# One kernel of convolutions, masked operations and filters: the next layer's code is read inside the running operation

## The chip, the cores and the metric

The kernel runs on one core of a Trainium2 chip. The core has TensorE (PE, matrix products, with its weight loads as PEld), VectorE (DVE), ScalarE (ACT), GpSimd (POOL) and SyncE (SP), each with its own stream of instructions; they meet at semaphores. The metric is the device time of one execution in microseconds (us), the median over runs.

## The reference

The input `x` has four images of 32 channels and 28 x 28 points in float32. Four stages follow one another, each a residual over a norm:

```python
x = x + conv_block(ln_channels(x))          # 1x1 and 3x3 convolutions, two L1-distance convolutions
t = to_tokens(x)                            # (4, 784, 32)
t = t + scan(ln_tokens(t))                  # 33 layers, see below
x = from_tokens(t)
x = x + quantised_convs(ln_channels(x))
t = to_tokens(x); t = t + spectral_filters(ln_tokens(t))
```

The change lies in the scan. Each of its 33 layers does this:

```python
op = argmax(h[0, 0, :19])                    # one token decides for all
y  = softmax(q @ k.T * scale) @ v @ wo[op]   # q, k, v = h @ wq[op], ...
h  = where(attn_mask[layer, op], y, h)
z  = relu(h @ w1[op] + b1[op]) @ w2[op] + b2[op]
h  = where(ffn_mask[layer, op], z, h)
```

The masks are mostly false, so that a layer may do nothing, an attention, an FFN, or both.

## The kernel before, in words

**Layout.** The four images lie side by side on the 128 partitions (32 channels each), the 784 points in the free dimension, mostly handled as two halves of 392. A product in float32 is two passes of PE, so the profile counts two per matmul. PSUM has eight banks.

**The scan as a program of jumps.** DVE keeps a table of which layers are active for which op. Once the first token of H is known, it works out the next active layer and its code (bit 0 attention, bit 1 FFN, above them the layer and the op) and writes it into KINT, one integer in SBUF: `decide` (L885 to L898, the last instruction a cast into KINT), which raises the semaphore `decided`. Before that it has made ready what can follow, in `past` and `look_ahead` (from L717 and L708). Every engine reads KINT into a register with a TENSOR_LOAD and jumps. `active_steps` builds the body of a layer, `step`, three times on each engine: for the first layer, the second, and in a loop for all further ones. With these inputs two layers are active: the first does an FFN only, so that PE, ACT and DVE jump over the attention's code, the second an attention and an FFN. Then the code is zero, and all jump to the exit.

**Around it on PE.** The LayerNorm ahead (`norm(1, ...)`) centres X1 by products with CEN, sums squares by products with VSEL, and spreads the reciprocal deviations RSC by eight products with CON and SPR; DVE multiplies them into H (L653). PE then waits for H, reads the code (L1249) and jumps. `keep_warm(n)` is n products of constants into an unused bank, which nobody reads; `bridge` is one product with a single column that carries a wait.

**The FFN.** A one-column product for the deciding token; eight hidden units HIDT (two halves by four images, numbers 0 to 7), each one product with W1R into a bank, evicted with bias and relu by ACT (0, 2, 3, 4, 6; L561) or DVE (1, 5, 7; L995); between units 3 and 4 the token's own row, from which DVE decides the next layer; then two groups of four output products with W2S (L1408 to L1410), which ACT evicts to the halves of H (L565). PE then adds two products CEN by X1 into banks 4 and 5, the first part of the third LayerNorm, should this layer be the last. SyncE waits for `decided`, and fetches the weights of the next operation: W4R (attention), W1R and W2S (FFN).

**The attention's end.** Scores, exponentials (ACT, PT), and products with the values VT run in fourteen steps. The sum of the exponentials (the denominator) comes from products with ones: DVE adds the first of a chunk in ACC (L965), PE sums the others and then ACC into bank 7. DVE takes the reciprocal (L981), PE multiplies the values' sum NUM by W4R, DVE scales the result into H (L984), and decides again.

Every engine has its order written out by hand; what runs when follows from these orders and the semaphores.

## Time and profile before

| | |
|---|---|
| median of 3 runs | 344.49 us (344.34 to 348.11) |
| profiled execution | 343.95 us, its span 342.2 us |
| PE busy | 322.1 us (94%), in 5173 passes |
| DVE, ACT busy | 249.4 us (73%), 188.6 us (55%) |
| granted clock of PE | nine tenths or more in all 40 slices |

Times in the trace count from the span's start. The span holds what the engines do; the rest of the execution lies around it. The scan starts at about 140 us and the third LayerNorm ends at about 232 us. A matmul's end is modelled, so PE counts as busy while passes are in flight.

### The profile page before, as it was taken

What the parts mean: (1) busy time and instruction counts of PE and PEld (TensorE: products, weight loads), DVE (VectorE), ACT (ScalarE), POOL (GpSimd) and SP (SyncE); (2) the same over time, 40 slices, a digit from 0 to 9 for tenths busy, and PEclk for the clock granted to TensorE, in tenths of its full rate; (3) what the DMA queues carried; (4) which work ended last, traced back from release to release, by engine and by line L of the source; (5) the groups of instructions that cost most, each with busy time, mean ns of one, the idle gap of its engine ahead of it and who ended that gap; (6) DMA issues with size and microseconds to landing.
All of it is one profiled execution on the core that took longest, in us unless ns stands there. A gap on an engine that the chain in (4) does not pass through costs nothing.

```text
span 342.2 us, 11955 instructions
## 1 busy us (share of the span) xinstructions
PE 322.1 (94%) x5173; PEld 202.4 (59%) x5173; DVE 249.4 (73%) x510; ACT 188.6 (55%) x214; POOL 21.5 (6%) x48
## 2 busy tenths in 40 slices
PE   8899799999999999958999999989899999999995
PEld 7436437763333333434465334446589999999984
DVE  2797999999999999544694877647657675564444
ACT  3871898887889894324584867641333323223221
POOL 4573000000000000300000000000000000000000
PEclk9999999999999999999999999999999999999999
DMA  5701820000000003700000000000023000000001
GB/s 181 234 17 20 310 99 2 2 1 2 2 2 2 2 2 111 268 14 19 3 0 2 3 1 2 2 5 1 2 61 87 7 4 4 4 5 4 6 4 50
DMA packets 12243, 13.20 MB, mean 39 GB/s; under 512 B 6026, under 2 KB 10908, under 8 KB 12184
## 3 DMA queue, kind: packets, MB, share of 16 engines
q1 hardware_dynamic: 11208, 9.17, 9.0%
q0 software_dynamic: 832, 3.00, 2.6%
q8 instruction: 43, 0.70, 0.9%
q10 hardware_dynamic: 144, 0.20, 0.2%
q14 instruction: 16, 0.13, 0.1%
HBM read 10.73 MB, written 0.40 MB: 33 GB/s over the span
## 4 chain that ended last, share of the span: by engine, by line
PE 54%; DVE 31%; SPq 7%; issue 4%; ACT 2%; DVEq 1%; DMA 1%; ACTq 0%
PE PS L1088 54%; DVE pool_ L877 18%; SPq L274 3%; DVE pool_ L965 1%; DVE TMP L841 1%; DVE TMP L973 1%; SPq L268 1%; DMA WA2R<-in_wa2r 1%; SPq L277 1%; SPq L279 1%; DVE RSC L648 1%; DVE pool_ L874 1%; SPq L281 1%; DVE MSC L790 1%; ACT pool_ L544 0%
## 5 line engine op out<-in xcount | busy, mean ns | idle before, releaser
L1088 PE MATMUL PS<-pool_,CON 128*32 128x392 f32 (+2 forms) x1320 | 111.4, 493 | 0.6 <-ACT pool_ L544 0.2
L1088 PEld LDWEIGHTS PS<-pool_,CON 128*32 128x32 f32 (+1 forms) x1320 | 49.0, 110 | 60.8 <-issue 43.7
L495 ACT ACTIVATE pool_<-TMP,WA 128x3136 f32<-128x3136 f32 x26 | 75.3, 2924 | 11.0 <-PE PS L1088 10.8
L877 DVE TENSOR_SCALAR pool_<-TMP,WA 128x3136 f32<-128x3136 f32 x44 | 79.4, 1845 | 0.1
L594 ACT ACTIVATE pool_<-PS 128x272 f32<-128x272 f32 x64 | 25.4, 398 | 56.7 <-PE PS L1088 56.6
L1061 DVE TENSOR_TENSOR pool_<-PS,pool_ 128x128 f32<-128x128 f32 x64 | 18.6, 290 | 35.4 <-PE PS L1088 32.7
L1088 PE MATMUL PS<-HE,WS 128*32 128x136 f32 (+1 forms) x768 | 36.7, 317 | 0.2 <-ACT WS L586 0.2
L1088 PE MATMUL PS<-pool_,WS 128*32 128x136 f32 (+1 forms) x768 | 36.7, 316 | 0.0
L1088 PEld LDWEIGHTS PS<-pool_,WS 128*32 128x32 f32 x768 | 28.7, 109 | 3.0
L1088 PEld LDWEIGHTS PS<-HE,WS 128*32 128x32 f32 x768 | 28.3, 110 | 3.6 <-issue 0.6
L1088 PE MATMUL PS<-pool_,TMP 128*32 128x128 f32 x512 | 29.0, 272 | 0.0
L1088 PE MATMUL PS<-CON 128*128 128x196 f32 (+1 forms) x112 | 21.7, 332 | 4.3 <-issue 3.8
L544 ACT ACTIVATE pool_<-PS 112x896 f32<-112x896 f32 (+1 forms) x28 | 21.5, 820 | 6.1 <-PE PS L1088 6.1
L1088 PEld LDWEIGHTS PS<-CON 128*128 128x128 f32 x112 | 18.1, 190 | 10.8 <-issue 8.4
L965 DVE TENSOR_TENSOR pool_<-pool_ 112x1792 f32<-112x1792 f32 (+1 forms) x9 | 16.3, 1810 | 5.1 <-ACT pool_ L544 5.0
L1088 PEld LDWEIGHTS PS<-pool_,TMP 128*32 128x32 f32 x512 | 18.9, 109 | 0.0
L1062 DVE TENSOR_TENSOR pool_<-PS,pool_ 128x136 f32<-128x136 f32 x64 | 18.5, 288 | 0.0
L1064 DVE TENSOR_TENSOR pool_<-PS,pool_ 128x128 f32<-128x128 f32 x64 | 17.9, 280 | 0.0
L1088 PE MATMUL PS<-QZ,Y 32*112 32x448 f32 (+1 forms) x112 | 15.2, 532 | 0.7 <-ACT pool_ L544 0.7
L944 DVE CUSTOM_DVE_ANT_0 pool_<-PS,pool_ 112x392 f32<-112x392 f32 x28 | 13.8, 561 | 2.3 <-ACT pool_ L525 2.3
L1088 PE MATMUL PS<-pool_,ASEG 128*32 128x49 f32 (+2 forms) x512 | 14.6, 247 | 0.2 <-DVE pool_ L1064 0.2
L1088 PE MATMUL PS<-Y,QZ 32*112 32x392 f32 x56 | 14.0, 529 | 0.0
(261 smaller groups left out, 372.3 us busy)
## 6 DMA issues: line engine op xcount, KB each, us to landing
pool_<-in_pho SPq DMA_DIRECT2D x1, 3144.0 KB, 10.7
HE<-in_phe SPq DMA_DIRECT2D x1, 3136.0 KB, 12.5
QZ<-CW SPq DMA_DIRECT2D x12, 98.0 KB, 2.4
CW<-in_cw POOLq DMA_DIRECT2D x2, 576.0 KB, 4.8
CON<-in_con POOLq DMA_DIRECT2D x1, 732.5 KB, 5.4
out_y<-Y SPq DMA_DIRECT2D x1, 392.0 KB, 2.4
CQ<-in_ws SPq DMA_DIRECT2D x16, 9.0 KB
MPP<-in_mpp POOLq DMA_DIRECT2D x1, 256.0 KB, 2.9
```

Of the source, the lines that this page charges most:

```text
L268: sp.dma_start(PAR[q, 0:PC["cb"]], rows_).then_inc(s["par_in"], 16)
L274: sp.dma_start(WS2N[32 * b + 8 * g:32 * b + 8 * g + 8, :, :], bass.AP(ws2.tensor, (32 * g + 8 * b) * 9 * P + C * b, [[9 * P, 8], [P, 9], [ ...
L495: a.activation(unit, window(n // CQ), ACT.Abs, bias=WA2[:, n:n + 1], scale=-1.0).then_inc(s["act_unit"], 1)
L544: a.activation(PT[0:QT, st % PR, 2 * pair:2 * pair + 2, 0:QC[ch]], PS[0:QT, 2 * ((u + 2) % 3):2 * ((u + 2) % 3) + 2, 0:QC[ch]], ACT.Exp, s ...
L594: a.activation(spans(UEV[:, u % 8, :], 2 * P), spans(PS[:, 2 * (u % 3), :], QE), ACT.Copy).then_inc(s["uev_act"], 1)
L877: v.tensor_scalar(unit, window(n // CQ), WA2[:, n:n + 1], None, ALU.max).then_inc(s["dve_unit"], 1)
L944: v.tensor_tensor_reduce(RISE[0:QT, j % 2, b, :], PS[0:QT, b, 0:HT], RISE[0:QT, j % 2, b, :], 1.0, -3.4e38, ALU.add, ALU.max, TOPS[0:QT, j ...
L965: v.tensor_tensor(ACC[0:QT, :, 0:w], PT[0:QT, (st - 1) % PR, :, 0:w] if i == 1 else ACC[0:QT, :, 0:w], PT[0:QT, st % PR, :, 0:w], ALU.add) ...
L1061: v.tensor_tensor(y[:, P:2 * P], low[:, 0:P], y[:, 0:P], ALU.add).then_inc(s["uev_sum"], 1)
L1062: v.tensor_tensor(y[:, 2 * P:NPH], low[:, 0:QE], y[:, 2 * P:NPH], ALU.add).then_inc(s["uev_sum"], 1)
L1064: v.tensor_tensor(y[:, P:2 * P], low[:, QE:QE + P], y[:, P:2 * P], ALU.add).then_inc(s["uev_dve"], 1)
L1088: return t.matmul(out_, lhsT, rhs, start=start, stop=stop, skip_group_check=True)
```

## The change

- **PE and ACT read the next code inside the FFN.** `next_code` stands between the two halves of the output and loads into a second register, `coming`; at the operation's end a register move takes it over. A layer without an FFN reads at its end, under a new condition. DVE and SyncE still read at the end of their step.
- **The first code** is read inside the LayerNorm: on PE after the variance's products, on DVE while it waits for the spreading products. PE's wait for H moves behind the jump, the wait for the evicted H of a layer before the next operation's first product, and for the last layer before the exit's first product.
- **The centring products of X1** move from behind the FFN to between its two output groups; each waits until the hidden unit in its bank is evicted.
- **ACT evicts six units** (0, 1, 2, 3, 4, 6), DVE two (5, 7), and DVE decides before them. The token's row stands after unit 1.
- **The attention's last products:** the sum over ACC comes before the last step's exponentials, which now finish the denominator; the two bridging products at the end become one of 32 columns; the token's row stands before the second output product.
- **Warming:** 3 products instead of 8 before the projections, 1 instead of 2 at the attention's end, and the 8 of the loop's layers go; two of the places use bank 7.
- **FFN code aligned:** the instructions after the first attention's code, where PE's jump over it lands, begin at a multiple of 256 instructions.

PE, the code read ahead of the first operation, before:

```order
L1088 MATMUL PS<-RSC,CON 128x98
L1088 MATMUL PS<-RSC,SPR 128x98
L1249 TENSOR_LOAD KINT [waits decided,ln_out]
L1250 REGISTER_ALU
L109 COMPARE_AND_BRANCH
L82 REGISTER_ALU
L82 COMPARE_AND_BRANCH
```

and now:

```order
L1099 MATMUL PS<-TMP,VSEL 32x98 x3
L1265 TENSOR_LOAD KINT [waits decided]
L1266 REGISTER_ALU
L1099 MATMUL PS<-X,CEN 128x392
L1099 MATMUL PS<-RSC,CON 128x98 [waits ln_rs]
L1099 MATMUL PS<-RSC,SPR 128x98
```

The read stands between the variance's products (TMP by VSEL) and the second centring product; only the branches are left behind the spreading products.

PE, the end of the first FFN, from the first output group on, before:

```order
L1088 MATMUL PS<-pool_,W2S 32x392 x3
L1406 REGISTER_ALU
L1407 REGISTER_ALU [waits hid_act]
L1088 MATMUL PS<-pool_,W2S 32x392 [waits hid_dve]
L1088 MATMUL PS<-pool_,W2S 32x392 x3
L1411 ISA
L1386 UNCONDITIONAL_BRANCH
L1412 ISA
L1088 MATMUL PS<-X,CEN 128x392 x2
L1418 ISA
L1419 REGISTER_ALU [waits ffn_h]
L1421 TENSOR_LOAD KINT [waits decided]
```

and now (the lines of the file have moved; CEN by X are the centring products):

```order
L1099 MATMUL PS<-pool_,W2S 32x392 [waits hid_act]
L1099 MATMUL PS<-pool_,W2S 32x392 x3
L1442 REGISTER_ALU
L1099 MATMUL PS<-X,CEN 128x392 [waits hid_act]
L1099 MATMUL PS<-X,CEN 128x392 [waits hid_dve]
L1273 ISA
L1275 TENSOR_LOAD KINT [waits decided]
L1447 REGISTER_ALU
L1449 REGISTER_ALU [waits hid_act]
L1099 MATMUL PS<-pool_,W2S 32x392 [waits hid_dve]
L1099 MATMUL PS<-pool_,W2S 32x392 x3
L1453 ISA
```

The centring products and the read stand between the two output groups; the wait for ffn_h is gone from here.

PE, the end of the attention, from the last step's sums on (pool_ by CON sums exponentials, pool_ by VT weighs the values, TMP by W4R is the output), before:

```order
L1088 MATMUL PS<-pool_,CON 32x336 [waits exp_done]
L1088 MATMUL PS<-pool_,CON 32x336 x3
L1361 REGISTER_ALU
L1088 MATMUL PS<-pool_,CON 32x336 [waits acc_done]
L1088 MATMUL PS<-pool_,CON 32x336 x3
L1088 MATMUL PS<-pool_,VT 32x336 x4
L1088 MATMUL PS<-CON 128x1 [waits att_scaled]
L1088 MATMUL PS<-TMP,W4R 32x448 x4
L1088 MATMUL PS<-CON 128x1 [waits num_out]
L1088 MATMUL PS<-TMP,W4R 32x336 x4
L1088 MATMUL PS<-W4R,TMP 1x32
```

and now:

```order
L1099 MATMUL PS<-pool_,CON 32x336 x3
L1099 MATMUL PS<-pool_,VT 32x336 x4
L1398 REGISTER_ALU
L1099 MATMUL PS<-pool_,CON 32x336 [waits acc_done]
L1099 MATMUL PS<-pool_,CON 32x336 x3
L1099 MATMUL PS<-pool_,CON 32x336 [waits exp_done]
L1099 MATMUL PS<-pool_,CON 32x336 x3
L1099 MATMUL PS<-pool_,VT 32x336 [waits att_scaled]
L1099 MATMUL PS<-pool_,VT 32x336 x3
L1099 MATMUL PS<-TMP,W4R 32x448 x4
L1099 MATMUL PS<-CON 32x1 [waits num_out]
L1099 MATMUL PS<-W4R,TMP 1x32
```

The sum over ACC (waits acc_done) stands first, the output's first group comes without a bridging product, the token's row (W4R by TMP) before the second group.

The core of the diff:

```diff
-WARM = dict(inputs=6, means=4, squares=2, deviations=3, scaled=4, sums=2, copies=9, evictions=3, shifts=1, relus=3, further=8, rises=2, weights=4, projections=8)
+WARM = dict(inputs=6, means=4, squares=2, deviations=3, scaled=4, sums=1, copies=9, evictions=3, shifts=1, relus=3, further=8, rises=2, weights=4, projections=3)
...
+            def next_code(more):
+
+                a.wait_ge(s["decided"], a.snap(ops, min_val=0, max_val=2 * NB) + more)
+                a.sem_inc(s["read_on"], 1)
+                a.load(coming, KINT[0:1, 0:1], bass_reorder=False)
...
-                    for u in (0, 2, 3, 4, 6):
+                    for u in (0, 1, 2, 3, 4, 6):
...
                     for h in range(2):
+                        if h:
+                            next_code(2)
                         a.wait_ge(s["ffn_out"], k * 2 + (h + 1))
                         a.activation(half(H, h), bank(2 + h), ACT.Identity, bias=B2C[:, :]).then_inc(s["ffn_h"], 1)
                     a.reg_add(nf, nf, 1); a.reg_add(ops, ops, 1)
-                a.wait_ge(s["decided"], a.snap(ops, min_val=1, max_val=2 * NB) + 1)
-                a.sem_inc(s["read_on"], 1)
-                a.load(code, KINT[0:1, 0:1], bass_reorder=False)
-                a.reg_mov(code, a.snap(code) & (OPW - 1))
+                with a.If((c & 2) < 1):
+                    next_code(1)
+                a.reg_mov(code, a.snap(coming) & (OPW - 1))
...
+            norm(1, X1, lambda h: half(H, h), after=first_code)
...
+                    decide(v.snap(ops, min_val=0, max_val=2 * NB) + 2, 7)
+                    for u in (5, 7):
                         v.wait_ge(s["ffn_h1"], k * 8 + (u + 1))
                         v.tensor_scalar(HIDT[:, u, :], bank(u % 7), B1S, 0.0, ALU.add, ALU.max).then_inc(s["hid_dve"], 1)
-                        if u == 1:
-                            decide(v.snap(ops, min_val=0, max_val=2 * NB) + 2, 7)
                     v.reg_add(nf, nf, 1); v.reg_add(ops, ops, 1)
...
+            norm(1, X1, "x1_ready", between=first_code)
...
-                with (t.If((c & 1) > 0) if built else far_unless(t, c & 1, ffn_mark)):
+                with (t.If((c & 1) > 0) if built else far_unless(t, c & 1, ffn_mark, align=True)):
                     k = t.snap(na, min_val=0, max_val=NB)
                     t.wait_ge(s["zeroed"], 4)
-                    keep_warm(WARM["projections"])
+                    keep_warm(WARM["projections"], b=7)
                     t.wait_ge(s["att_w"], k * 16 + 16)
+                    t.wait_ge(s["ffn_h"], t.snap(nf, min_val=0, max_val=NB) * 2 + 1)
+                    if not built:
+                        t.wait_ge(s["ln_out"], 4)
...
-                        if i > ADDS[ch]:
+                        if i > ADDS[ch] and not (ch == 1 and i == NQ - 1):
                             sums(PT[:, st % PR, :, :], i == ADDS[ch] + 1, False)
+                        last_ch = ch == 1
                         if i == NQ - 1:
-                            t.wait_ge(s["acc_done"], k * ADDED[2] + ADDED[ch + 1])
-                            sums(ACC, False, True).then_inc(s["den_done"], 1)
+                            if last_ch:
+                                sums(PT[:, st % PR, :, :], False, True).then_inc(s["den_done"], 1)
+                                t.wait_ge(s["att_scaled"], k + 1)
+                            else:
+                                t.wait_ge(s["acc_done"], k * ADDED[2] + ADDED[ch + 1])
+                                sums(ACC, False, True).then_inc(s["den_done"], 1)
                         for b in range(NIMG):
                             last = mm(bank(6, QC[ch], slice(32 * b, 32 * b + 32)), VT[0:QT, b, C * i:C * i + C],
                                       PT[0:QT, st % PR, b, 0:QC[ch]], i == 0, i == NQ - 1)
                         last.then_inc(s["pv_done"], 1)
+                        if st == 2 * NQ - 2:
+                            t.wait_ge(s["acc_done"], k * ADDED[2] + ADDED[2])
+                            sums(ACC, False, False)
...
-                    t.wait_ge(s["att_scaled"], k + 1)
                     for ch in range(2):
                         if ch:
                             t.wait_ge(s["num_out"], k * 2 + 2)
-                        bridge()
+                            mm(PS[0:C, 3, 0:1], CON[:, 0:C], CON[:, 0:1])
+                            token(NUM[0:C, 0:1], W4R[0:C, 3, :], 6)
                         for b in range(NIMG):
                             q = slice(32 * b, 32 * b + 32)
                             last = mm(bank(ch, QC[ch], q), W4R[q, 3, :], NUM[q, Q0[ch]:Q0[ch] + QC[ch]])
                         last.then_inc(s["att_wo"], 1)
-                    token(NUM[0:C, 0:1], W4R[0:C, 3, :], 6)
                     keep_warm(WARM["sums"])
...
+                        if u == 1:
                             t.wait_ge(s["ffn_wb"], k * 16 + 16)
                             t.wait_ge(s["tok_hid"], k + 1)
...
-                        t.wait_ge(s["hid_act"], k * 5 + 2 * h + 3)
-                        t.wait_ge(s["hid_dve"], k * 3 + 2 * h + 1)
+                        if h:
+                            t.wait_ge(s["hid_act"], k * 6 + 5)
+                            mm(bank(4), CEN[:, :], half(X1, 0), True, False)
+                            t.wait_ge(s["hid_dve"], k * 2 + 1)
+                            mm(bank(5), CEN[:, :], half(X1, 1), True, False)
+                            next_code(2)
+                        t.wait_ge(s["hid_act"], k * 6 + 2 * h + 4)
+                        if h:
+                            t.wait_ge(s["hid_dve"], k * 2 + 2)
                         for b in range(NIMG):
                             last = mm(PS[32 * b:32 * b + 32, 2 + h, 0:HT], W2S[:, 0:C], HIDT[:, 4 * h + b, :])
                         last.then_inc(s["ffn_out"], 1)
                     t.reg_add(nf, nf, 1); t.reg_add(ops, ops, 1)
-                f, o = t.snap(nf, min_val=0, max_val=NB), t.snap(ops, min_val=1, max_val=2 * NB)
-                built.append(o)
-                if len(built) == 3:
-                    keep_warm(WARM["further"])
-                for h in range(2):
-                    mm(bank(4 + h), CEN[:, :], half(X1, h), True, False)
-                t.wait_ge(s["ffn_h"], f * 2 + 1)
-                t.wait_ge(s["decided"], o + 1)
-                t.sem_inc(s["read_on"], 1)
-                t.load(code, KINT[0:1, 0:1], bass_reorder=False)
-                t.reg_mov(code, t.snap(code) & (OPW - 1))
+                with t.If((c & 2) < 1):
+                    for h in range(2):
+                        mm(bank(4 + h), CEN[:, :], half(X1, h), True, False)
+                    next_code(1)
+                built.append(c)
+                t.reg_mov(code, t.snap(coming) & (OPW - 1))
 
             active_steps(t, code, step, exit_marks, align=True)
 
+            t.wait_ge(s["ffn_h"], t.snap(nf, min_val=0, max_val=NB) * 2 + 1)
             for h in range(2):
                 mm(bank(4 + h), CEN[:, :], half(H, h), False, True).then_inc(s["sx_cent"], 1)
             t.wait_ge(s["sx_sq"], 2)
```

## Rows read from the trace of the kernel before

**Rows 1.** The page's chain of waits, whole span, shares by engine.
```profile
PE 54%; DVE 31%; SPq 7%; issue 4%; ACT 2%; DVEq 1%; DMA 1%; ACTq 0%
```
**Rows 2.** Windows: length, busy of PE, PEld, DVE, ACT, POOL, granted clock, DMA.
```profile
147.00:162.40 15.40, 10.59 (x68) 6.54 (x69) 6.77 (x19) 5.27 (x9) 0.00 (x0) 1.00 0.06 13
```
**Rows 3.** Timeline, first operation: start, us, engine, line, operation, [idle before <-releaser].
```profile
144.40 0.46 PE L1088 MATMUL PS<-RSC,CON 128*128 128x98 f32 x2 [0.44 <-DVE RSC L648]
...
146.47 0.56 DVE L653 TENSOR_TENSOR H<-TMP,PS 128x392 f32<-128x392 f32 x1 [0.33 <-PE PS L1088]
148.18 0.14 DVE L717 TENSOR_SCALAR PINT<-KINT 1x1 int32<-1x1 int32 x1 [1.15 <-issue]
...
149.48 1.56 PE L1088 MATMUL PS<-CON 128*128 128x196 f32 x8 [3.05 <-issue]
...
150.97 0.81 PE L1088 MATMUL PS<-H,W1R 32*128 32x1 f32 x3
...
151.76 0.15 DVE L992 COPY B2C<-W1R 128x1 f32<-128x1 f32 x1 [1.17 <-issue]
152.58 0.94 PE L1088 MATMUL PS<-H,W1R 32*128 32x392 f32 x7 [0.79 <-issue]
...
154.08 0.15 DVE L890 TENSOR_REDUCE KMAX<-PS 1x1 f32<-1x19 f32 x1
...
154.84 0.14 DVE L896 CAST KINT<-KMAX 1x1 int32<-1x1 f32 x1
...
156.37 0.87 PE L1088 MATMUL PS<-pool_,W2S 128*32 128x392 f32 x8 [0.73 <-DVE pool_ L995]
...
156.63 0.69 SPq L311 DMA_DIRECT2D W4R<-in_aw  x1
...
159.46 3.01 PE L1088 MATMUL PS<-CON 128*128 128x196 f32 x18 [0.71 <-issue]
...
162.40 2.84 PE L1088 MATMUL PS<-H,W4R 32*32 32x392 f32 x32
```
**Rows 4.** Tile KINT, code reads: engine, operation, ns min/median/max, first and last start.
```profile
L1421 PEldq TENSOR_LOAD <-KINT x2: 312/312/313, 158.2 to 224.6; - x2
...
L1249 PEldq TENSOR_LOAD <-KINT x1: 487/487/487, 147.1 to 147.1; - x1
```
**Rows 5.** DMA queues from 149 to 153 us: kind, packets, MB, share of 16 engines.
```profile
q8 instruction: 1, 0.02, 2.1%
```
**Rows 6.** DMA issues of the whole span: queue, count, KB each, median us to landing.
```profile
QZ<-CW SPq DMA_DIRECT2D x12, 98.0 KB, 2.4
...
W2S<-in_fwb SPq DMA_DIRECT2D x2, 16.5 KB, 2.2
```
**Rows 7.** Timeline, the attention's last products, PE and DVE.
```profile
213.51 1.34 PE L1088 MATMUL PS<-pool_,CON 112*32 112x336 f32 x16 [0.18 <-ACT pool_ L544]
...
215.34 0.38 PE L1088 MATMUL PS<-CON 128*128 128x1 f32 x2
...
217.69 0.51 DVE L984 TENSOR_TENSOR H<-TMP,PS 128x336 f32<-128x336 f32 x1 [0.51 <-PE PS L1088]
```
**Rows 8.** Timeline, the second FFN and the exit, PE and ACT.
```profile
218.77 1.14 PE L1088 MATMUL PS<-H,W1R 32*128 32x1 f32 x10 [0.26 <-issue]
...
219.95 2.50 ACT L561 ACTIVATE pool_<-PS,W2S 128x392 f32<-128x392 f32 x5 [0.51 <-PE PS L1088]
...
219.99 0.21 PE L1088 MATMUL PS<-CON,W1R 32*1 32x32 f32 x2
...
223.62 1.58 PE L1088 MATMUL PS<-X,CEN 128*128 128x392 f32 x4
223.76 0.59 ACT L565 ACTIVATE H<-PS,B2C 128x392 f32<-128x392 f32 x1 [0.62 <-PE PS L1088]
224.93 1.28 ACT L574 ACT_TABLE_LOAD   x1 [0.58 <-issue]
...
226.67 0.50 ACT L407 ACTIVATE TMP<-PS 128x392 f32<-128x392 f32 x1 [0.24 <-PE PS L1088]
```

More of the change, by code:

```diff
@@ L906, in _, with first_code @@
             decide(1, 6)
-            norm(1, X1, lambda h: half(H, h))
+            code = v.alloc_register("v_code"); na = v.alloc_register("v_na"); nf = v.alloc_register("v_nf")
+            def first_code():
+                v.wait_ge(s["decided"], 1)
+                v.load(code, KINT[0:1, 0:1], bass_reorder=False)
+                v.reg_mov(code, v.snap(code) & (OPW - 1))
+            norm(1, X1, lambda h: half(H, h), after=first_code)
             def residual():
                 v.tensor_tensor(X[:, :], X1[:, :], H[:, :], ALU.add).then_inc(s["x2_ready"], 1)
-            code = v.alloc_register("v_code"); na = v.alloc_register("v_na"); nf = v.alloc_register("v_nf")
-            v.wait_ge(s["decided"], 1)
-            v.load(code, KINT[0:1, 0:1], bass_reorder=False)
-            v.reg_mov(code, v.snap(code) & (OPW - 1))
             ops = v.alloc_register("v_ops")
@@ L1113, in spread, with norm @@
                 return last
-            def norm(k, src, ready=None, summed=None):
+            def norm(k, src, ready=None, summed=None, between=None):
                 if k == 1:
@@ L1142, in norm @@
                 last.then_inc(s["ln_var"], 1)
+                if between:
+                    between()
                 rest(k)
@@ L1244, in _, with first_code, next_code @@
             ffn_mark = t.mark_branch_hint_location()
[L1245 to L1247 removed]
             code = t.alloc_register("t_code"); na = t.alloc_register("t_na"); nf = t.alloc_register("t_nf")
[L1249 to L1252 removed]
+            ops = t.alloc_register("t_ops"); coming = t.alloc_register("t_coming")
             built = []
[L1254 removed]
+            def first_code():
+                t.wait_ge(s["decided"], 1)
+                t.load(code, KINT[0:1, 0:1], bass_reorder=False)
+                t.reg_mov(code, t.snap(code) & (OPW - 1))
+                t.reg_mov(na, 0); t.reg_mov(nf, 0); t.reg_mov(ops, 0); t.reg_mov(coming, 0)
+            norm(1, X1, "x1_ready", between=first_code)
+            def next_code(more):
+                t.wait_ge(s["decided"], t.snap(ops, min_val=0, max_val=2 * NB) + more)
+                t.sem_inc(s["read_on"], 1)
+                t.load(coming, KINT[0:1, 0:1], bass_reorder=False)
             exit_marks = []
```

35 lines of the change are left out of this document (14 added, 21 removed).

## The prediction

> **What bounds the kernel now.** I read the page's chain first: PE holds 54% of it and VectorE (DVE) 31%, "issue" only 4% [rows 1]. Nearly all of that PE share lies in stages that the change does not touch. The diff touches the data-dependent part: the second LayerNorm, an FFN (the first operation), an attention, an FFN, and the exit into the third LayerNorm. So I read busy time by stretch next. From 147.0 to 162.4 us PE works 10.6 of 15.4 us at a granted clock of 1.00 [rows 2]: this is the stretch with holes, nearly 5 us of them, and a part of what is busy there is warming. Then I read this stretch and the one from 213 us to the exit in order of time [rows 3, 7, 8] and the reads of the decided code by their tile [rows 4]. The reader is to see there that PE starts its first FFN product at 150.97, 3.9 us after its input H is complete (146.47 + 0.56), and the first projection of the attention at 162.40, 4.5 us after H is complete again. Those two delays are what the change can take; the attention from 162.4 to 213.5 us stays as it is, apart from its last products.
>
> **First operation, PE's start.** Now H is complete at 147.03, PE's sequencer reads the code (0.49 us [rows 4]), runs register operations and two branches, and the first warming product comes at 149.48: 2.45 us, after a hole of 3.05 us [rows 3]. In the change the read stands after the variance products and nothing but the branches follows the last spreading product. What does the read cost in its new place? At least nothing; at most 0.49 us plus its share of the 1.9 us of register work, some 1.2 us in all. PE idles 0.44 us before the spreading products at 144.40, and the centring product ahead of them pipelines into them, so I take 0.25 us, which also delays H to 147.3. What is gained: the sequencer runs ahead of the array (its later read begins at 224.6 while the products of 223.62 run to 225.20 [rows 4, 8]), so the branches hide under the spreading products, which end at 146.4. The warming products can start at 146.5 to 146.7 instead of 149.48, last 1.5 us, and the token product starts at 148.1 to 148.3 instead of 150.97. Had the sequencer no lead, the start would be 149.8. I take 148.2: **2.8 us earlier**.
>
> **The code gap.** Inside the FFN PE stops for 0.79 us, until 152.58, on nothing but "issue" [rows 3], half a dozen products behind the far branch; one instruction transfer falls into 149 to 153 us on queue q8 [rows 5]. In the second FFN, reached without a far branch, the same products run without a hole (ten passes in 1.14 us) [rows 8]. The aligned code lies in one fetch block, so I take the gap as gone; its bounds are 0 and 0.8 us, and here it is worth less than that, since DVE becomes the later engine, as follows.
>
> **DVE and the decision.** DVE's look-ahead starts at 148.18, after a gap of 1.15 us that holds its own code read; B2C is copied at 151.76, 3.6 us later; the decision takes 0.9 us (154.08 to 154.98) [rows 3]. Its read moves under the wait for the spreading products, so the look-ahead starts between 147.3 and 148.2; I take 147.5. That gives B2C at 151.1 and, because the token's row is now ready at 149.7 (1.5 us after the token product, as from 218.77 to 219.99 + 0.21 [rows 8]) and no eviction stands before it, the decision at 151.3 to 152.3 instead of 154.98: **2.7 us earlier**. SyncE issues the attention weights W4R 1.65 us after a decision (154.98 to 156.63) [rows 3]. How long they take to land has no row. SyncE's transfers of 16.5 and 98 KB took 2.2 and 2.4 us [rows 6]; for these 64 KB I take 2.4, nearest the larger, with 2.0 and 3.0, a little outside both rows, as bounds: W4R is there at 156.4.
>
> **The new order at the FFN's end.** ACT evicts six units instead of five, at 0.5 us each (five in 2.50 us [rows 8]): it starts 1.2 us after the token product and ends at +4.25, not +3.7. The first output products need four of them, at +3.3. Then come the two centring products of X1 (1.58 us), which now stand **before** the second output products; the later one needs DVE's unit 5, evicted right behind the decision, for which I take 0.2 us and the 0.59 us of ACT's eviction of as many elements [rows 8]: 153.1. So the second output products start at about 154.0 (PE's own order would give 148.2 + 5.7 = 153.9), against 156.37 now; they take 0.87 us and ACT 0.59 for H, complete at 155.6 [rows 3, 8]. The read between the halves costs 0.31 us on the sequencer [rows 4] under the centring products: nothing. What stood between the halves' end and the projection, centring 1.58, read and branches, and sixteen passes of warming (with a bridge 2.94 us [rows 3]), shrinks to branches that hide under ACT, and six passes: 1.1 us, from 155.1 to 156.2. The projection then waits for W4R at 156.4 and one bridging product of 0.3 to 0.4 us: 156.8 instead of 162.40, **5.6 us saved**. Bounds: 6.3 (DVE early, W4R in 2.0 us) and 2.9 (PE's start not earlier, below).
>
> **The attention's tail.** The sum over ACC moves into PE's wait for the last exponentials (idle 0.18 us by its row, plus the turn of the following group [rows 7]): 0.2 to 0.4 us. The first bridging product (0.38 us at 215.34) goes; the second is replaced by a small product and the token's, about as long. One warming product fewer ends behind att_h and is free. DVE's H product at 217.69, and with it the second FFN's start at 218.77, come 0.6 us earlier, less 0.1 us for one more wait: **0.5 us saved**, bounds 0.2 and 0.7.
>
> **The exit.** Here the new order loses. Counted from the token product at 218.77, H is now complete at +5.6 (223.76 + 0.59), with the centring pair behind it. In the change the second output products start at +5.7, behind the centring pair, and H is complete at +7.2. Then ACT must load the Sqrt table: 1.28 us, then a dummy of 0.20, before the squares. Now that load starts at 224.93 and hides under centring and PE's code read; the squares start at 226.67, or +7.90 [rows 8]. In the change it starts at +7.2 to +7.5 and the squares at +8.75 to +9.05. The cover was the centring pair behind the output, and it is gone. **0.95 us lost**, bounds 0.6 and 1.3. PE itself would be ready at +7.25, so what is late next is ACT.
>
> Sum: 5.6 + 0.5 − 0.95 = 5.1 us. The profiled execution took 343.95 us for a span of 342.2, 0.54 below the median of 344.49; 343.95 − 5.1 = 338.9, and against the median 339.4. I say **339.3**.
>
> **Two rules weighed.** The first hole, 3.05 us of idle PE at 149.48, left the granted clock at 1.00 [rows 2, 3], its 2.4 GHz level, and the change shortens the holes. The Trainium skill, "TensorE: Matmul & The Clock Gate", What's actually happening, says that the throttled state is PE's default and activity alone lifts it, which speaks against dropping ten warming passes; by it the third rival would come true, by the row the sum stands. The far branch: PE ran from its target at 149.48, and stopped until 152.58 [rows 3]. The Trainium skill, "Runtime: NRT & Kernel Launch", Instruction fetch mechanics, says that a taken branch out of the fetched window waits for a transfer of the target block; this is the first rival, whose time is worked out from rows alone.
>
> **Rivals.** (1) *The branch outruns its code.* The target block was there at 149.4, but no row says that it is there at 146.5. If PE's first FFN starts no earlier than now, at 150.97, the decision falls at 153.4, the second output products at 156.6, H at 158.1, warming from 158.0 to 159.2, and the projection at 159.5: 2.9 us saved instead of 5.6, 341.5 in all with tail and exit; with the gap left too, 342.5. For it: the hole of 0.79 us is of this kind. Against: the prefetch hint still stands before the LayerNorm. Chance 0.17. (2) *Everything at its good end*: 6.3 + 0.7 − 0.6 = 6.4, so 337.6 to 338.1; beyond 337.6 lies the line of 2% (6.9 us), about what a measurement of this kernel can tell from no change. Chance 0.13, of which I give 0.10 to the far side. (3) *Slower*: with five warming products fewer the granted clock falls to 1.2 GHz ahead of the projections. The price is the PE work on the chain at that level once more: the projections alone hold 2.84 us [rows 3], and from 5.1 us of such work on the gain is used up; if it lasts 8 us the time is 342, through the whole 18 us of first scores 357. Against: the change leaves no hole longer than 1.2 us there. Chance 0.05, 0.03 of it beyond 2%. (4) *The change doesn't move the path*: DVE's look-ahead and the W4R transfer, not PE, release the projection. That is already so in my sum, and only fixes it at 156.8. The forecast keeps 0.65.
>
> **Numbers.** 339.3; the range 337.3 to 342.3 takes in the forecast's bounds and the first rival without its gap. Faster by over 2%: 0.10. Slower by over 2%: 0.03. Within: 0.87.
>
> **What would show it.** In the changed profile: PE's warming products 0.1 to 0.4 us after the last spreading product and none of the FFN's products after an "issue" hole; KINT's second cast near 152.2; the first W4R product near 156.8; the sum over ACC before the last exponentials; the centring pair between the FFN's two output groups; and at the exit ACT's table load right behind H, with squares 8.75 to 9.05 us after the token product, PE idle before. The prediction is wrong if PE's first FFN still starts near 151, if the projection waits for something other than W4R, or if the granted clock leaves 1.00.

## The result

The changed kernel takes 342.29 us (median of 5 runs, 340.68 to 348.47) against 344.96 us (5 runs of the kernel before): ratio 0.9899, 95% interval 0.9863 to 0.9935. The profiled execution took 340.68 us, 3.27 us less than that of before, and its span is 338.9 us against 342.2. 339.3 was forecast, with a range from 337.3 to 342.3.

The chain of waits, in the form of [rows 1]:

```profile
PE 58%; DVE 28%; SPq 7%; issue 3%; ACT 2%; DMA 1%; ACTq 0%; DVEq 0%
```

The first operation in order of time, as in [rows 3], and below it the window's busy times and clock, as in [rows 2]:

```profile
144.53 0.37 PE L1099 MATMUL PS<-RSC,CON 128*128 128x98 f32 x2
...
147.65 1.56 PE L1099 MATMUL PS<-CON 128*128 128x196 f32 x8 [1.18 <-issue]
149.14 1.14 PE L1099 MATMUL PS<-H,W1R 32*128 32x1 f32 x6
150.51 1.58 PE L1099 MATMUL PS<-H,W1R 32*128 32x392 f32 x12
151.85 0.14 DVE L904 CAST KINT<-KMAX 1x1 int32<-1x1 f32 x1
153.38 1.58 PE L1099 MATMUL PS<-X,CEN 128*128 128x392 f32 x4
153.65 0.69 SPq L311 DMA_DIRECT2D W4R<-in_aw  x1
154.90 0.87 PE L1099 MATMUL PS<-pool_,W2S 128*32 128x392 f32 x8
155.70 1.38 PE L1099 MATMUL PS<-CON 128*128 128x196 f32 x8
157.00 1.19 PE L1099 MATMUL PS<-H,W4R 32*32 32x392 f32 x12
```

```profile
147.60:157.00 9.40, 8.86 (x58) 4.95 (x58) 6.03 (x16) 4.89 (x10) 0.00 (x0) 1.00 0.04 11
```

The projections start at 157.00 instead of 162.40: **5.40 us saved**, with PE busy for 8.86 of 9.40 us and the clock at 1.00. The longest hole left, 1.18 us on "issue", lies ahead of that window, between the spreading products and the warming behind the jump.

The attention's end, the second FFN and the exit, as in [rows 7, 8]:

```profile
207.66 1.31 PE L1099 MATMUL PS<-pool_,CON 112*32 112x336 f32 x16
209.47 0.95 PE L1099 MATMUL PS<-TMP,W4R 32*32 32x448 f32 x8
211.38 0.50 DVE L996 TENSOR_TENSOR H<-TMP,PS 128x336 f32<-128x336 f32 x1
212.46 1.14 PE L1099 MATMUL PS<-H,W1R 32*128 32x1 f32 x6 [0.64 <-DVE H L996]
213.63 3.17 ACT L568 ACTIVATE pool_<-PS,W2S 128x392 f32<-128x392 f32 x6 [0.51 <-PE PS L1099]
216.70 1.58 PE L1099 MATMUL PS<-X,CEN 128*128 128x392 f32 x4
218.22 0.87 PE L1099 MATMUL PS<-pool_,W2S 128*32 128x392 f32 x8
219.15 0.59 ACT L574 ACTIVATE H<-PS,B2C 128x392 f32<-128x392 f32 x1 [1.73 <-PE PS L1099]
219.79 1.58 PE L1099 MATMUL PS<-H,CEN 128*128 128x392 f32 x4 [0.71 <-ACT H L574]
222.12 1.28 ACT L582 ACT_TABLE_LOAD   x1 [2.38 <-issue]
223.52 0.87 ACT L407 ACTIVATE TMP<-PS 128x392 f32<-128x392 f32 x2
```

From the first projection to the second FFN's token product it takes 55.46 us, before 56.37: **0.91 saved**. From there to the squares at the exit 11.06 us (223.52 − 212.46), before 7.90: **3.16 lost**. Together 3.15, against 3.3 in the span. The row to stop at is the table load: H is complete at 219.74, nothing is released any more, and yet ACT does nothing for 2.38 us. Before, that gap was 0.58 [rows 8].

The granted clock of single runs lies between 0.97 and 1.00, in the kernel before down to 0.98, and moves a run by some microseconds; so the experiments are read by stage, counted from the first spreading product (144.53 in the changed kernel) or the token product.

### The profile page after: what moved, and what is told of

It is laid out like the page before. It is cut to its first block, busy times and chain, and to the rows that moved or that the text cites. A ratio compares the mean times of both kernels' runs of the same rounds, so it can differ in the third digit from the quotient of the medians.

```text
span 338.9 us, 11933 instructions
## 1 busy us (share of the span) xinstructions
PE 319.3 (94%) x5159; PEld 201.5 (59%) x5159; DVE 248.3 (73%) x508; ACT 189.6 (56%) x216; POOL 21.3 (6%) x48
## 4 chain that ended last, share of the span: by engine, by line
PE 58%; DVE 28%; SPq 7%; issue 3%; ACT 2%; DMA 1%; ACTq 0%; DVEq 0%
PE PS L1099 58%; DVE pool_ L885 18%; SPq L274 3%; DVE TMP L849 1%; SPq L268 1%; SPq L277 1%; SPq L279 1%; DMA WA2R<-in_wa2r 1%; DVE pool_ L882 1%; SPq L281 1%; DVE MSC L798 1%; DVE RSC L656 0%; DVE ASEG L803 0%; DVE CW L820 0%; DVE WMX L707 0%
## 5 line engine op out<-in xcount | busy, mean ns | idle before, releaser
L1099 PEld LDWEIGHTS PS<-pool_,WS 128*32 128x32 f32 x768 | 30.1, 109 | 2.2
L1099 PEld LDWEIGHTS PS<-HE,WS 128*32 128x32 f32 x768 | 29.4, 110 | 3.2 <-issue 0.6
L1099 PE MATMUL PS<-pool_,TMP 128*32 128x128 f32 x512 | 30.2, 272 | 0.0
L1099 PE MATMUL PS<-CON 128*128 128x196 f32 (+2 forms) x98 | 19.2, 332 | 1.7 <-issue 1.2
L1099 PEld LDWEIGHTS PS<-CON 128*128 128x128 f32 (+1 forms) x98 | 15.6, 188 | 8.3 <-issue 5.8
L1099 PEld LDWEIGHTS PS<-pool_,TMP 128*32 128x32 f32 x512 | 20.1, 108 | 0.0
```

Source lines behind the costliest of these rows:

```text
L1099: return t.matmul(out_, lhsT, rhs, start=start, stop=stop, skip_group_check=True)
```

## What holds the exit

**Theory:** ACT's jump to the exit, past the loop of further layers, lands on code that has not been fetched, since its code has grown; the fetch is what the forecast left out. **Rival:** the gap belongs to the table load or the late H.

*act_exit_hint* announces the jump, as VectorE and TensorE do:

```diff
+                if len(begun) == 2:
+                    exit_marks.append(a.mark_branch_hint_location())
...
-            active_steps(a, code, step)
+            active_steps(a, code, step, exit_marks)
```

> One edit: ScalarE too announces its jump out of the loop of operations, with a branch hint at the head of its second step, as VectorE and TensorE do. Theory (code fetch): in the changed kernel ScalarE ends the last eviction into H at 219.74, and its table load for Sqrt starts only at 222.12, 2.38 us later, with nothing released in between; that time is the fetch of the code behind the jump. With the hint the idle time falls to 0.3 to 0.6 us, the first squares start at token product + 9.0 to 9.4 instead of + 11.06 (the table load, 1.28 us, stays exposed), and the run is 1.7 to 2.1 us shorter than the changed kernel's, some 338.7 on its own clock. Rival (the load or the late H): the 2.38 us belong to the table load or to the long wait for H; then the hint changes nothing, idle 2.2 to 2.5 and squares at + 11.0, time within 0.3 us of the changed kernel's. Second rival: the hint is given over 60 us ahead and is lost by then; nothing changes either, and a hint nearer the jump would tell the two apart.

*act_reads_late* puts only ACT's read back to the step's end, without a hint:

```diff
-                        if h:
-                            next_code(2)
...
-                with a.If((c & 2) < 1):
-                    next_code(1)
-                a.reg_mov(code, a.snap(coming) & (OPW - 1))
+                a.wait_ge(s["decided"], a.snap(ops, min_val=1, max_val=2 * NB) + 1)
+                a.sem_inc(s["read_on"], 1)
+                a.load(code, KINT[0:1, 0:1], bass_reorder=False)
+                a.reg_mov(code, a.snap(code) & (OPW - 1))
```

> Only ScalarE's reading of the coming layer's code goes back to where it was before the change: at the step's end, behind the second eviction into H, once for both operations. Its code is then about as long as before the change, so that the code behind the loop lies where it did. Theory A (layout): ScalarE's wait at its jump depends on where in its code the jump and its target lie; with the old layout the idle time between the last H and the table load falls from 2.38 us to the 0.5 to 0.9 of before, and the read (0.28 us) and its register moves come back on the path of H to the jump; the squares start at token product + 9.2 to 9.9 instead of + 11.06. Theory B (the jump's time alone): the wait starts when the jump is reached whatever the layout, since a jump out is never fetched ahead; then squares stay at + 11.0 to 11.6. First operation: nothing on TensorE hangs on ScalarE's read, projections at 157.0 plus or minus 0.2.

ACT's last eviction into H and the table load, with the hint, and then with the late read:

```profile
219.44 0.59 ACT L580 ACTIVATE H<-PS,B2C 128x392 f32<-128x392 f32 x1 [1.72 <-PE PS L1105]
220.52 1.28 ACT L588 ACT_TABLE_LOAD   x1 [0.50 <-issue]
```

```profile
219.81 0.59 ACT L572 ACTIVATE H<-PS,B2C 128x392 f32<-128x392 f32 x1 [1.73 <-PE PS L1098]
220.98 1.28 ACT L581 ACT_TABLE_LOAD   x1 [0.58 <-issue]
```

The gap falls from 2.38 to 0.50 and 0.58 us, though H is as late and the load is the same. The squares start 9.19 and 9.26 us after the token product instead of 11.06. So the rival falls: 1.9 us of the loss are the jump, and the hint takes them away. In the changed kernel ACT's branch to the exit (L117) stands at 219.6 and takes 0.05 us itself; the wait lies behind it, and the queues show a code transfer inside the gap, from 219.6 to 222.2 us:

```profile
q14 instruction: 1, 0.01, 1.3%
```

With the hint there is none from 219.5 to 221 us. That the place of the code decides is argued and not shown: act_reads_late changes the code's length, the time of the read and a branch at the step's end all at once. A hint given 63 us ahead is still good. (The Trainium skill, "Runtime: NRT & Kernel Launch", Instruction fetch mechanics, says that a taken branch to a page outside the fetched window waits for its transfer; this trace agrees, with 1.9 us here.) act_exit_hint ran at 0.9857 of the time of before (0.9814 to 0.9901), act_reads_late at 0.9823 (0.9792 to 0.9855); the profiled executions took 339.35 and 339.39 us, 1.3 less than the changed kernel's.

*hint_table* also loads the Sqrt table in the attention's tail:

```diff
+                    a.activation(WSM[:, 45:46], con_("eps6", 1), ACT.Sqrt)
                     sums_out(1)
```

> Three edits on ScalarE, meant as the fastest version: the branch hint for its jump out of the loop; a dummy Sqrt near the attention's end, ahead of the eviction of the last sums, where ScalarE is idle for 1.63 us, so that the Sqrt table is loaded there and not behind the last eviction into H; the dummy Exp stands ahead of the two copies of the projections instead of behind them, which keeps its table load at the head of the attention. Theory: behind the last eviction into H only the jump and a dummy activation of 0.20 us are left, squares at token product + 8.0 to 8.6 instead of + 11.06, and the attention's tail is unchanged as the load and dummy (1.48 us) fit into the idle 1.63; 2.4 to 3.0 us shorter than the changed kernel, some 337.9. Rival (no fetch): the table moves but the wait before it stays, squares at + 9.7 to 10.0, gain 1.1 to 1.4. Where the dummy does not fit, the tail is up to 0.5 us longer.

ACT's timeline; the last line is the first half of the squares:

```profile
208.29 1.28 ACT L561 ACT_TABLE_LOAD   x1
...
220.56 0.20 ACT L589 ACTIVATE WSM<-CON 128x1 f32<-128x1 f32 x1 [0.52 <-issue]
221.05 0.50 ACT L407 ACTIVATE TMP<-PS 128x392 f32<-128x392 f32 x1 [0.29 <-PE PS L1106]
```

The squares come at +8.30, released by PE and no longer by ACT. The exposed load cost 0.89 us. The profiled execution took 338.70 us, and the run 0.9872 of the time of before (0.9827 to 0.9917).

*centring_last* puts the centring pair of X1 behind the second output products again, on top of that:

```diff
-                            t.wait_ge(s["hid_act"], k * 6 + 5)
-                            mm(bank(4), CEN[:, :], half(X1, 0), True, False)
...
                         last.then_inc(s["ffn_out"], 1)
+                    for h in range(2):
+                        mm(bank(4 + h), CEN[:, :], half(X1, h), True, False)
```

> The version hint_table with one more edit: in the FFN the two centring products of X1 stand behind the second output products again, as before the change, while the code is still read between the halves. Theory: the second output products start 1.5 us earlier in both FFNs. In the second FFN H is complete at token product + 5.7 instead of + 7.28, the centring pair (1.58 us) runs while ScalarE evicts and jumps, and the squares start at token product + 7.2 to 7.6, against + 8.30 in hint_table and + 7.90 before the change: 0.7 to 1.1 us shorter than hint_table at the exit. In the first FFN nothing is won, since W4R releases the projections in hint_table (a wait for it of 0.39 us): 157.2 to 157.6 there. Together some 337.6 at full clock against 338.5. Rival (the pair between the halves costs nothing at the exit, or its new place delays the last products into the centring): squares at + 8.1 to 8.6, no gain; or TensorE's later warming delays the projections by 0.3 to 0.5, which takes half the gain away.

The exit on PE and ACT, from the second output products to the squares:

```profile
218.40 0.87 PE L1106 MATMUL PS<-pool_,W2S 128*32 128x392 f32 x8 [0.16 <-ACT pool_ L575]
219.19 1.58 PE L1106 MATMUL PS<-X,CEN 128*128 128x392 f32 x4
...
221.47 0.50 ACT L407 ACTIVATE TMP<-PS 128x392 f32<-128x392 f32 x1 [0.83 <-PE PS L1106]
```

With the token product at 213.93 the squares stand at +7.54, 0.76 earlier than in hint_table and 0.36 earlier than before the change: the new order's own price is that 0.76. The fastest run took 337.68 us at a clock of 1.00, the median 339.26, which is 0.9843 of before (0.9803 to 0.9883). 11.06 − 7.54 is thus 1.87 of jump, 0.89 of table load, 0.76 of order.

## What holds the first operation

**Theory**, as in the forecast: VectorE's decision and then W4R release the projections. **Rival:** PE's own chain does, since its jump outruns its code (the forecast's first rival).

*look_twice* doubles VectorE's reduction of 0.79 us:

```diff
-                v.tensor_reduce(NEXT[0:1, :], lk, AX.X, ALU.max)
-                v.drain()
+                for _ in range(2):
+                    v.tensor_reduce(NEXT[0:1, :], lk, AX.X, ALU.max)
+                    v.drain()
```

> VectorE's longest look-ahead instruction, the reduction of 0.79 us over LOOK, is issued twice, with a drain behind each; nothing else is changed. In the changed kernel the projections start at 157.00, with TensorE's warming products right ahead of them, and W4R was issued at 153.65. Theory (two chains nearly level, VectorE's close behind TensorE's): the decision moves from 152.0 to 152.8, the issue of W4R from 153.65 to about 154.45, and the projections to 157.6 to 158.0, with a wait for W4R ahead of them; that is 0.6 to 1.0 us later and not less, since W4R is at most 0.5 us ahead of TensorE now. Rival (TensorE alone bounds, with W4R long there): projections at 157.0 to 157.2.

```profile
154.84 0.69 SPq L311 DMA_DIRECT2D W4R<-in_aw  x1
157.58 0.30 PEld L1100 LDWEIGHTS PS<-CON 128*128 128x128 f32 x2 [0.38 <-issue]
157.89 0.15 PEld L1100 LDWEIGHTS PS<-H,W4R 32*32 32x32 f32 x8
```

Counted from the spreading products, which stand 0.29 later here, the issue of W4R is 0.90 later and the projections 0.60: W4R was at most 0.3 us ahead in the changed kernel. (The profile puts the wait ahead of the bridging product down to "issue"; that it is W4R's is read from the 0.60.) The margin depends on the landing, which varies: by the DMA rows W4R's last bytes arrive 2.30 us after the issue in look_twice, 2.55 in the changed kernel and 2.70 in hint_table, and where the projections wait for them, they start 0.75 to 0.85 behind. In the changed kernel's profiled execution W4R would have released the projections at 156.95 to 157.05, level with PE's 157.00. The other side shows in hint_table, where PE's hole happens to be shorter, and W4R becomes the releaser, 3.2 us after its issue at 153.75:

```profile
147.29 1.56 PE L1106 MATMUL PS<-CON 128*128 128x196 f32 x8 [0.72 <-issue]
156.99 0.38 PE L1106 MATMUL PS<-CON 128*128 128x1 f32 x2 [0.39 <-DMA W4R<-in_aw]
```

And where the hole is longer, the projections follow it one for one: 1.46 us in act_exit_hint and act_reads_late instead of 1.18, projections 12.76 and 12.75 us after the first spreading product instead of 12.47. With the same hole they stay at 12.47 in hint_early (below), though W4R lands 0.25 us sooner after its issue there. So **PE's chain releases them, with W4R between level and 0.3 us ahead**, and the hole is on the path: a longer one costs all that it adds, a shorter one gains only until W4R holds.

What sets the hole? *hint_early* gives PE's hint before the convolution's last nine groups:

```diff
+                if n == 9 * CQ - 9:
+                    ffn_mark = t.mark_branch_hint_location()
```

> Only TensorE's hint for its jump past the first attention's code is given earlier, before the last nine groups of the convolution instead of behind them and the warming products. In the changed kernel TensorE's warming products start at 147.65, 1.18 us after the row products with nothing released in between, where 0.2 to 0.3 were forecast. Theory: the block with the code of the second FFN lands late (rival 1 of the prediction in part); with an earlier hint the wait falls by 0.7 to 1.0 and the token product comes at about 148.2 to 148.5 instead of 149.14, while the projections stay at 157.0 plus or minus 0.2, since VectorE's look-ahead and the landing of W4R release them: run time within 0.3 us of the changed kernel's. Rival: TensorE's own chain sets the projections; then they start 0.7 to 1.0 us earlier and the run is that much shorter. Second rival: the block is brought at its own time whatever the hint, warming stays at 147.6.

The hint comes at 122.8 instead of 137.0, and nothing moves, as the second rival says: a hole of 1.18 us, projections at 157.01; over all 0.9904 of before (0.9850 to 0.9959). The next expectation says 4 us earlier; it was 14. *no_pe_hint* takes the hint away:

```diff
-            ffn_mark = t.mark_branch_hint_location()
...
-                with (t.If((c & 1) > 0) if built else far_unless(t, c & 1, ffn_mark, align=True)):
+                with (t.If((c & 1) > 0) if built else far_unless(t, c & 1, None, align=True)):
```

> TensorE's jump past the first attention's code stays, aligned as in the changed kernel, but without a branch hint. With the hint given 4 us earlier the warming products behind the jump started at 147.64, as in the changed kernel (147.65): so the hint's place does not time the code's arrival. Theory (the hint does bring the block, at a time of its own): without it the transfer starts only when the jump is reached, and the wait ahead of the warming products grows from 1.18 to 2 us or more; the first product of the FFN at 150 or later, the projections later by as much. Rival (the hint does nothing here): 1.2 to 1.5 us, token product at 149.1 to 149.5, projections at 157.0 to 157.3, as in the kernels with it.

PE behind the jump, and the clock of two windows:

```profile
149.42 2.95 PE L1101 MATMUL PS<-CON 128*128 128x196 f32 x8 [3.06 <-issue]
```

```profile
142.00:147.60 5.60, 3.67 (x36) 2.53 (x34) 3.19 (x8) 2.23 (x4) 0.00 (x0) 1.00 0.21 53
150.00:154.00 4.00, 4.00 (x14) 2.77 (x12) 0.15 (x1) 0.26 (x1) 0.00 (x0) 0.50 0.02 6
```

The hole grows by 1.9 us, and behind it the clock is at 1.2 GHz, so that the warming takes 2.95 us instead of 1.56; the profiled run took 351.22 us. From 143 to 147.5 us queue q8 carries two transfers of code here, in the kernels with the hint one:

```profile
q8 instruction: 2, 0.03, 3.4%
```

The jump itself (the first of the two branches of L82 on PE's sequencer; ns, then first and last start) in the kernel before, in the changed one and without the hint:

```profile
L82 PEldq COMPARE_BRANCH  x2: 360/371/382, 148.7 to 225.3; - x2
L82 PEldq COMPARE_BRANCH  x2: 348/1292/2235, 145.0 to 217.9; - x2
L82 PEldq COMPARE_BRANCH  x2: 353/2286/4218, 144.8 to 228.5; - x2
```

The sequencer comes to the jump at 145.0, ahead of the array as forecast, and then the jump takes 2.24 us, without the hint 4.22. In the kernel before it was reached at 148.7 and took 0.38: there the one transfer from 143 to 149.5 us had begun at 143.7, 5 us ahead. So the hint spares a transfer, but the one that is left starts no earlier, and the new order reaches the jump before its code. *pad_code* tests whether the code's place in its block times it, with 64 more instructions ahead:

```diff
+                if g >= 16:
+                    t.wait_ge(s["con_in"], 16)
```

> TensorE's code ahead of the jump is made 64 instructions longer, with one more wait, on a semaphore that has long been raised, ahead of each of the convolution's last 64 groups; nothing else is changed. Hint or no hint, early or late, one 16 KB transfer of TensorE's code began between 144.6 and 145.4 us in each of the kernels so far, and the warming products behind the jump came 2.7 to 3.0 us after it. Theory (the transfer starts where TensorE's code crosses into another block, so its place in the program times it): 64 instructions more bring that crossing ahead of the read of the code; the transfer starts at 143.5 or earlier, counted on the changed kernel's clock, and the warming products follow the row products with a hole of 0.5 us or less instead of 1.18, token product at 148.0 to 148.5 instead of 149.14; the projections, then released by W4R, at 156.9 to 157.4. Rival (the jump itself starts the transfer): 1.0 to 1.7 us of hole as in the others, transfer at 144.6 or later. The 64 waits take some 0.05 us of TensorE's sequencer each and may cost the convolution up to 0.5 us; that is read apart.

A miss for my theory: the hole is 1.45 us, and the transfer begins, as in all the changed versions, within about 0.4 us of the time at which PE's sequencer comes to the jump. Over the twelve of them that keep the hint the hole ranges from 0.72 to 1.71 us, with the length of that transfer (0.93 to 1.43 us in the trace) and its start. What triggers the transfer just there stays open.

*no_align* leaves out the aligning, *warm8* puts eight warming products back:

```diff
-                with (t.If((c & 1) > 0) if built else far_unless(t, c & 1, ffn_mark, align=True)):
+                with (t.If((c & 1) > 0) if built else far_unless(t, c & 1, ffn_mark)):
```

> The changed kernel without the aligning of TensorE's FFN code behind the jump (the hint stays). Theory of the prediction (the aligned code lies in one block): the hole of 0.79 us among the FFN's first products, which the kernel before had and the changed one has not, comes back, 0.5 to 1.2 us with nothing released in between; as TensorE's chain sets the projections by up to 0.4 us, they start 0.3 to 0.9 us later, 157.3 to 157.9. Rival (the hole went because the products come later, when the next block has landed): no hole, projections at 156.8 to 157.3.

```diff
-WARM = dict(..., weights=4, projections=3)
+WARM = dict(..., weights=4, projections=8)
```

> Only the number of warming products ahead of the projections goes back from three to eight (sixteen passes and the bridge instead of six and the bridge). In the changed kernel TensorE's warming starts at 155.70, lasts 1.38 us in eight passes, and the projections follow at 157.00. Theory (the warming stands on the path, W4R at most 0.5 us ahead): ten more passes of 0.16 us, projections 1.3 to 1.7 us later, at 158.3 to 158.7, and the run by as much longer. Rival (W4R or the decision bounds): projections at most 0.9 us later. On the clock: with three products the granted clock was 1.00 through the projections in the changed kernel; the five more change nothing of that in either theory.

Without aligning, the FFN's products up to the first output group show no hole on "issue":

```profile
148.70 1.14 PE L1099 MATMUL PS<-H,W1R 32*128 32x1 f32 x6
150.07 1.62 PE L1099 MATMUL PS<-H,W1R 32*128 32x392 f32 x12
152.14 0.87 PE L1099 MATMUL PS<-pool_,W2S 128*32 128x392 f32 x8 [0.46 <-ACT pool_ L568]
155.26 1.45 PE L1099 MATMUL PS<-CON 128*128 128x196 f32 x8
156.64 0.85 PE L1099 MATMUL PS<-H,W4R 32*32 32x392 f32 x6
```

From the token product to the warming ahead of the projections it takes 6.56 us, as with the aligning, and the projections stand 12.42 us after the spreading products (12.47 with it): here the aligning is worth nothing, and why the gap of before went stays open. With eight warming products they stand at 14.16, 1.69 later: the shorter warming is on the path in full.

*short_start* leaves one warming product of four ahead of the FFN, on top of centring_last:

```diff
-WARM = dict(..., weights=4, projections=3)
+WARM = dict(..., weights=1, projections=3)
```

> The version centring_last with one more edit: behind TensorE's jump into the first FFN one warming product stands instead of four. There the products of the FFN stood behind the warming (148.22, 1.56 us), while their input H was complete at 147.1; the projections followed the warming ahead of them at 157.61, not a wait for W4R. Theory (two chains nearly level): the token product starts 1.1 us earlier, at 148.5 to 148.8, but the decision (VectorE, 152.0) and with it W4R stay where they are; the projections come 0.2 to 0.5 us earlier, 157.1 to 157.4, with a short wait for W4R or for VectorE's units ahead of them, and the run is that much shorter, some 337.4 at full clock. Rival 1 (TensorE alone sets the projections): the whole 1.1 us is won, projections at 156.5. Rival 2 (the clock): with a hole of 1.2 to 1.7 us ahead and less warming, the granted clock falls behind the jump, the FFN's products take about twice as long, and the projections come over 1 us later than in centring_last, as in the kernel without the hint.

```profile
149.41 2.76 PE L1106 MATMUL PS<-H,W1R 32*128 32x392 f32 x12
152.09 2.08 PE L1106 MATMUL PS<-pool_,W2S 128*32 128x392 f32 x16
156.73 0.53 PE L1106 MATMUL PS<-H,W4R 32*32 32x392 f32 x4
```

The theory and the second rival came in part: the token product is 1.54 us earlier (counted from the spreading products), the clock falls (0.82 from 147.6 to 157 us; 2.76 us for products that took 1.59), and the projections are still 0.74 earlier, of which 0.54 is a shorter hole at the jump (1.17 us instead of 1.71). The runs show nothing of it: the fastest took 337.73 us at a clock of 1.00, against 337.68, and the medians are 339.31 and 339.26.

*tail_before* undoes the attention's last products:

```diff
-                            if last_ch:
-                                sums(PT[:, st % PR, :, :], False, True).then_inc(s["den_done"], 1)
+                            t.wait_ge(s["acc_done"], k * ADDED[2] + ADDED[ch + 1])
+                            sums(ACC, False, True).then_inc(s["den_done"], 1)
```

> Only the attention's last products are back in the order of before: the sum over ACC behind the last exponentials, both bridging products of full size, and the token's product of W4R behind them. Theory: from the first projection to the second FFN's token product the changed kernel takes 55.46 us, the kernel before 56.37; with the order undone the whole 0.9 us comes back, 56.2 to 56.45, and nothing else moves. Rival: 0.4 or more of the 0.9 us came from elsewhere in the attention (the step's code read, the shorter warming); then 55.7 to 55.95.

```profile
208.55 1.34 PE L1099 MATMUL PS<-pool_,CON 112*32 112x336 f32 x16 [0.18 <-ACT pool_ L551]
210.70 0.95 PE L1099 MATMUL PS<-TMP,W4R 32*32 32x448 f32 x8
213.92 0.60 PE L1099 MATMUL PS<-H,W1R 32*128 32x1 f32 x2 [0.69 <-DVE H L996]
```

From the projections (157.52) to the token product 56.40 us: the 0.9 us is the order's own.

## Why the prediction held, and where it did not

- **The sum.** 5.1 us forecast, 3.3 measured in the profiled executions. The first operation gave 5.40 for 5.6, the tail 0.91 for 0.5, and the exit took 3.16 for 0.95, so the error of the exit is cancelled only in small part. That the median of 342.29 still lies in the range, 0.01 us below its upper end, is luck: this end was worked out for the first rival, a late start of PE, and not for a dearer exit.
- **The failed step: the exit.** "0.95 us lost, bounds 0.6 and 1.3" measured 3.16. H late by 1.70 (+7.28 instead of +5.58) and the exposed table load were in the sum. Missing was ACT's jump: I let the load follow H at once, though the row of before had 0.58 us on "issue" ahead of it [rows 8], and though the change alters ACT's code around it. The load started at +9.66 instead of +7.2 to +7.5. With the hint the squares come at +9.19, near the forecast's 8.75 to 9.05: the late H and the exposed load were sized about right.
- **PE's start** was forecast at 146.5 to 146.7 and came at 147.65. This is the first rival in part: the branch does outrun its code, by 1.18 us, not by all that the early read gains. It cost little, for W4R would have held the projections at most 0.3 us earlier.
- **Who releases the projections.** W4R in the forecast, at 156.8; PE's chain in fact, at 157.00, which the forecast itself had named as a sign that it is wrong. The time was right within 0.2 us because the two chains are nearly level, which is luck too. The decision came at 152.0, within 152.3, and W4R's bytes landed within my bounds of 2.0 and 3.0 us; left out were some 0.5 us from the last bytes to the bridging product that waits for them (3.2 us from the issue in hint_table).
- **The new order at the FFN's end:** second output products at 154.90, not 154.0, the late start carried on; from the token product +5.76, as forecast (+5.7).
- **The code gap** went, as forecast, but not by the aligning, as no_align shows.
- **The tail:** 0.91, over my bound of 0.7. From the last exponentials' end to the W4R products it is 0.70 us shorter (209.47 − 207.97 against 210.70 − 208.50); the rest lies in the products behind. I had counted the bridging product and the sum's place as partly the same time.
- **The clock** stayed at 1.00 up to the projections; the third rival did not come in the changed kernel, though the clock did fall in no_pe_hint and short_start. The rival's price was summed wrongly: if 8 us of work cost 8 us more, the time is 347, not 342.

## What to carry to other kernels

Count a jump like an operation: on every engine that takes one, ask where its target lies and whether a hint announces it, above all when a change brings that engine to the jump sooner or alters its code around it. Two chains that arrive within 0.3 us of each other turn a correct total into a coin toss on the cause, so lengthen each by itself to see which one holds. A cover that a reordering takes away (centring over a table load) should be replaced in the same change: the idle 1.6 us on ACT in the attention's tail took that load for nothing.

## What the runs showed of the hardware that I had not expected

- A branch hint is worth 1.9 us on ACT and on PE here, and giving it 14 us earlier on PE makes no difference. In the changed versions PE's transfer begins only about when the jump is reached; in the kernel before it had begun 5 us ahead.
- After a hole of 3.05 us before the change the clock was 1.00 [rows 2, 3]; after one of 3.06 in no_pe_hint it was at 1.2 GHz, and in short_start a hole of 1.17 with less warming behind it was enough. The length of the hole alone does not tell.
